# A graph layer's table build: four buffer places, x in seven groups, counts on two engines, stores on another queue

## The reference

```
f = layernorm(x) @ W_n                      # 6250 x 256, as 8 heads x 32
el, er = f . attn_l, f . attn_r             # per node 8 heads x 4 types
e  = leaky(((el[src] + er[dst] + edge16 . attn_m) . edge4) / 3)     # 200000 edges, sorted by dst
x  = x + segment_sum(f[src] * segment_softmax(e, dst), dst)
x  = x + mixture of 8 experts, best 2 of them, of layernorm(x)      # silu(h w1) * (h w3), w2
```

## Time and profile before

| what | us |
|---|---|
| median of 3 runs (4030.01 to 4046.42) | 4033.45 |
| the profiled execution, by its own time | 4042.06 |
| its span, first to last instruction | 4040.5 |
| VectorE, ACT, POOL, TensorE busy | 1992.2, 1598.6, 1860.2, 2976.2 |
| mean granted TensorE clock | 0.800 of full |

### The profile page before, as it was taken

One profiled execution on the slowest core, in us unless ns is written; L12 is line 12 of the kernel. 1 busy time (PEld: TensorE's weight loads), 2 busy tenths in 40 slices (PEclk: granted clock), 3 DMA queues, 4 the chain that ended last, 5 costly groups with the idle time before them and its releaser, 6 DMA issues. The chain is left out here.

```text
span 4040.5 us, 59260 instructions
## 1 busy us (share of the span) xinstructions
PE 2976.2 (74%) x12566; PEld 2283.4 (57%) x12567; DVE 1992.2 (49%) x5348; ACT 1598.6 (40%) x3631; POOL 1860.2 (46%) x1906
## 2 busy tenths in 40 slices
PE   2541677777777777767767777777665999999997
PEld 1221565555556666556555555656553677777775
DVE  5730566565655666556555565655782222222221
ACT  2310554544455455445445544544432222222221
POOL 0006466666666666666666666666163111111111
PEclk9765678787777777877778777767755999999998
DMA  7844444444445444444445444446555121121223
GB/s 219 269 140 115 116 135 134 131 136 135 132 135 145 133 133 134 135 132 135 134 134 143 135 135 132 134 134 123 120 188 176 31 31 31 31 31 31 31 31 83
DMA packets 309415, 481.35 MB, mean 119 GB/s; under 512 B 161911, under 2 KB 237507, under 8 KB 300366
## 3 DMA queue, kind: packets, MB, share of 16 engines
q0 software_dynamic: 100848, 285.40, 28.4%
q1 hardware_dynamic: 194910, 181.82, 14.9%
q10 hardware_dynamic: 13392, 11.23, 1.0%
HBM read 408.52 MB, written 76.12 MB: 120 GB/s over the span
## 5 line engine op out<-in xcount | busy, mean ns | idle before, releaser
L821 POOL DMA_INDIRECT rows<-table,idx x1664 | 1577.9, 948 | 981.3 <-issue 462.6
L864 PE MATMUL ps_acc<-rows,hot 128*128 128x264 f32 x3328 | 1217.8, 497 | 352.3 <-issue 158.2
L864 PEld LDWEIGHTS ps_acc<-rows,hot 128*128 128x128 f32 x3328 | 715.4, 238 | 456.3 <-issue 334.2
L849 PEld LDWEIGHTS ps_term<-er,hot_t 128*128 128x128 f32 x3328 | 607.2, 239 | 217.7 <-issue 155.1
L849 PE MATMUL ps_term<-er,hot_t 128*128 x3328 | 566.9, 300 | 91.3 <-issue 67.6
L1153 DVE TENSOR_TENSOR rows<-rows,ps_p 128x512 f32<-128x512 f32 x832 | 565.9, 680 | 6.0 <-ACT ps_p L973 0.5
L962 ACT ACTIVATE hot<-iota_row,neg_rel 128x128 f32<-128x128 f32 x1664 | 545.6, 388 | 5.5 <-PE ps_acc L864 5.5
L1736 PE MATMUL ps_h<-w,acc 128*128 x1680 | 528.5, 457 | 0.5 <-ACT acc L1655 0.5
L1648 POOL DMA_INDIRECT x_dram<-acc,to x105 | 161.8, 1541 | 761.9 <-ACT acc L1664 761.9
L1169 DVE TENSOR_TENSOR acc<-acc,ps_acc 128x264 f32 x832 | 354.9, 427 | 312.0 <-issue 171.4
L945 ACT ACTIVATE hot_t<-dst_row,neg_part 128x1024 f32<-128x1024 bf16 x208 | 235.6, 1133 | 520.4 <-remote 430.4
(11 more groups left out here) (263 smaller groups left out, 2827.1 us busy)
## 6 DMA issues: line engine op xcount, KB each, us to landing
dst_row<-rel_d SPq DMA_DIRECT2D x52, 1024.0 KB
rows<-table,idx POOLq DMA_INDIRECT x1664
rec<-rec_d SPq DMA_DIRECT2D x832, 24.0 KB
rec_d<-acc SPq DMA_DIRECT2D x16, 1050.0 KB
acc<-slots_x SPq DMA_DIRECT2D x105, 130.0 KB, 2.1
acc<-in_edge_attr_dram SPq DMA_DIRECT2D x16, 700.0 KB
wrow<-in_L_ffn_w_dram ACTq DMA_DIRECT2D x16, 640.0 KB
table<-fo SPq DMA_DIRECT2D x49, 148.0 KB
```

The lines of the kernel that those rows point to most:

```text
L821: pool.indirect_dma_start(rows[:, in_ring(k) + j, :], None, table, bass.IndirectOffsetOnAxis(ap=idx[w][:, t:t + 1], axis=0)).then_inc(gath ...
L849: last = pe.matmul(ps_term[s % 2][:, t * HT:(t + 1) * HT], hot_t[s % 2][:, t, :], flat(er[:, ds(b, 1), :]), start=False, stop=(t == QT - 1))
L864: last = pe.matmul(ps_acc[(k1 - 1) % SUM_BANKS][:, 0:PW], hot[m // QI % 2][:, m % QI * G + j, :], rows[:, in_ring(i * (2 * NI) + at) + j, ...
```

## The change

- `AHEAD` = 4 places for `xt`, `xn`, `fo` and `ps_f`, `TURNED` = 3 for `ps_t`, with waits that let each engine run as far ahead as there are places.
- x comes in seven groups of seven blocks (`load_x`), each with its own semaphore, statistics (`spread`), square root (`root`) and reciprocal (`roots`), the later ones inside the loop over blocks.
- The counts of odd blocks run on ACT: the sum over sign(thr - 0.5 - dst), which the next stage turns into a count by 0.5 s + 800. Those of even blocks stay on VectorE.
- Row stores and chunk stores are issued by POOL, on its own queue. SP's program holds loads alone; its order is x group 0, weights, router rows, dst, x group 1, src, chunks 0 and 1, x groups 2 to 6, chunks 2 to 15.
- One chunk for every three blocks (`chunk_after`).
- All loops are written out; before, they were loops of the engines' sequencers.

The diff, cut to its core:

```diff
-EARLY = 5
+AHEAD = 4
+TURNED = 3
+CHUNK_EVERY = 3
+ACT_COUNTS = range(1, BLOCKS, 2)
...
+            xt = sb(st, "xt", [P, AHEAD, KC, P])
+            xn = sb(st, "xn", [P, AHEAD, DIM])
+            fo = sb(st, "fo", [P, AHEAD, FD])
             ps_w = ps(st, "ps_w", [P, 512])
-            ps_t = [ps(st, f"ps_t{i}", [P, 512]) for i in range(2)]
-            ps_f = [ps(st, f"ps_f{i}", [P, 512]) for i in range(2)]
+            ps_t = [ps(st, f"ps_t{i}", [P, 512]) for i in range(TURNED)]
+            ps_f = [ps(st, f"ps_f{i}", [P, 512]) for i in range(AHEAD)]
...
+            def chunk_after(b):
+
+                c, left = divmod(b, CHUNK_EVERY)
+                return c if left == 0 and c < CHUNKS else None
...
+                    for b in range(BLOCKS):
+                        pool.wait_ge(f_sb, b + 1)
+                        pool.dma_start(table[b * P:(b + 1) * P, :], fo[:, b % AHEAD, :]).then_inc(f_out[b % AHEAD], 16)
+                        c = chunk_after(b)
+                        if c is not None:
+                            pool.wait_ge(rec_ok, c + 1)
+                            for part_of in SPREAD:
+                                pool.dma_start(rec_d[0:EDGES, :].rearrange("(p t) c -> p (t c)", p=EP)[part_of, c * CHUNK * RC:(c + 1) * CHUNK * RC],
+                                               rec_o[c % 2][part_of, :]).then_inc(rec_out[c % 2], 16)
+                    for u in range(AHEAD):
+                        pool.wait_ge(f_out[u], 16 * len(range(u, BLOCKS, AHEAD)))
+                    for u in range(2):
+                        pool.wait_ge(rec_out[u], 32 * (CHUNKS // 2))
...
+                    def load_x(g):
+
+                        lo, hi = g * BC, (g + 1) * BC
+                        if g == GROUPS - 1:
+                            hi -= 1
+                            sp.wait_ge(dve_step, 4)
+                            sp.dma_start(xall[0:LAST, hi, :], x[hi * P:NODES, :]).then_inc(x_in[g], 16)
+                        sp.dma_start(xall[:, lo:hi, :], x[lo * P:hi * P, :].rearrange("(b p) d -> p b d", p=P)).then_inc(x_in[g], 16)
+
+                    def load_chunk(c):
+                        u = c % 2
+                        if c >= 2:
+                            sp.wait_ge(rec_ok, c - 1)
+                        for tile, edge in ((e16_st[u], edge16), (e4_st[u], edge4)):
+                            f = edge.shape[1]
+                            for part_of in SPREAD:
+                                sp.dma_start(tile[part_of, :], edge.rearrange("(p t) f -> p (t f)", p=EP)[part_of, c * CHUNK * f:(c + 1) * CHUNK * f]).then_inc(chunk_in[u], 16)
+
+                    load_x(0)
+                    sp.dma_start(wall[:, :, 0:DIM], w_n.rearrange("(k p) d -> p k d", p=P)).then_inc(w_in, 16)
+                    sp.dma_start(rt_rows[:, :], router_w).then_inc(w_in, 16)
+                    sp.wait_ge(dst_none, 4)
                     sp.dma_start(dst_sb[0:1, 1:COLS + 1], dst[0:COLS].unsqueeze(0)).then_inc(dst_in, 16)
                     for lo, hi in ((1, 113), (113, EP)):
                         sp.dma_start(dst_sb[lo:hi, :], bass.AP(dst.tensor, lo * COLS - 1, [(COLS, hi - lo), (1, COLS + 1)])).then_inc(dst_in, 16)
-                    xv = x[0:(BLOCKS - 1) * P, :].rearrange("(b p) d -> p b d", p=P)
-                    sp.dma_start(xall[:, 0:BLOCKS - 1, :], xv).then_inc(x_in, 16)
-                    sp.dma_start(wall[:, :, 0:DIM], w_n.rearrange("(k p) d -> p k d", p=P)).then_inc(w_in, 16)
-                    sp.dma_start(rt_rows[:, :], router_w).then_inc(w_in, 16)
-                    sp.wait_ge(dve_step, 4)
-                    sp.dma_start(xall[0:LAST, BLOCKS - 1, :], x[(BLOCKS - 1) * P:NODES, :]).then_inc(x_in, 16)
+                    load_x(1)
...
+                    for c in range(2):
+                        load_chunk(c)
+                    for g in range(2, GROUPS):
+                        load_x(g)
+                    for c in range(2, CHUNKS):
+                        load_chunk(c)
...
+                    def root(g):
+
+                        act.wait_ge(var_ok, g + 1)
+                        act.activation(rstd[:, g * BC:(g + 1) * BC], mv[:, g * BC:(g + 1) * BC, 1], ACT.Sqrt, bias=eps[:, 0:1]).then_inc(std_ok, 1)
+
+                    root(0)
...
+                        if b >= AHEAD:
+                            act.wait_ge(f_ps, b - AHEAD + 1)
+                        act.copy(xt[:, b % AHEAD, :, :], ps_t[b % TURNED][:, 0:KC * P].rearrange("p (k n) -> p k n", k=KC)).then_inc(xt_sb, 1)
...
+                    def count(b):
+
+                        act.activation(junk_a, dst_sb[:, 1:COLS + 1], ACT.Sign, bias=thr_a[:, b:b + 1], scale=-1.0,
+                                       accum_out=cnt[:, b + 1:b + 2]).then_inc(signs_ok, 1)
+
+                    act.wait_ge(pad_ok, 2)
+                    act.dma_start(rec_d[EDGES:EDGES + PAD, :].rearrange("(a n) c -> a n c", a=64), pad_rec[:, :, :]).then_inc(pads, 16)
+                    copy_xt(0)
+                    copy_xt(1)
                     act.wait_ge(rec_zero, 2)
                     act.wait_ge(src_in, 32)
                     act.wait_ge(pen_ok, 1)
-                    copy_xt(0, 0)
-                    copy_xt(1, 1)
-                    for c in range(2):
-                        pack(0, c)
-                        for u in range(2):
-                            next_xt(2 * c + 2 + u, u)
-                    with act.Fori(1, CHUNKS // 2) as j:
-                        for c in range(2):
-                            pack(j, c)
-                            for u in range(2):
-                                next_xt(j * 4 + (2 * c + 2 + u), u)
-                    with act.Fori(2 * CHUNKS + 2, BLOCKS - 1, 2) as b:
-                        for u in range(2):
-                            next_xt(b + u, u)
-                    act.wait_ge(f_ps, BLOCKS - 2)
-                    copy_xt(BLOCKS - 1, 0)
+                    for b in range(BLOCKS):
+                        if b + 2 < BLOCKS:
+                            copy_xt(b + 2)
+                        if b % BC == 0 and b // BC + 1 < GROUPS:
+                            root(b // BC + 1)
+                        c = chunk_after(b)
+                        if c is not None:
+                            pack(c)
+                        if b in ACT_COUNTS:
+                            act.wait_ge(signs_ok, ACT_COUNTS.index(b))
+                            count(b)
...
+                    def spread(g):
+
+                        at = slice(g * BC, (g + 1) * BC)
+                        dve.wait_ge(x_in[g], 32 if g == GROUPS - 1 else 16)
+                        for b in range(g * BC, (g + 1) * BC):
+                            dve.bn_stats(stats[:, b, :], xall[:, b, :]).then_inc(stats_ok, 1)
+                        dve.wait_ge(stats_ok, BC * (g + 1))
+                        join_stats(dve, dve_steps, stats[:, at, :], mv[:, at, :], tmp[:, at, :], var_ok, g + 1)
+
+                    def roots(g):
+
+                        at = slice(g * BC, (g + 1) * BC)
+                        dve.wait_ge(std_ok, g + 1)
+                        dve_steps(dve.reciprocal(rstd[:, at], rstd[:, at]))
+
+                    def norm(b):
+                        if b >= AHEAD:
+                            dve.wait_ge(xt_ps, b - AHEAD + 1)
+                        dve.tensor_scalar(xn[:, b % AHEAD, :], xall[:, b, :], mv[:, b, 0:1],
+                                          rstd[:, b:b + 1], ALU.subtract, ALU.mult).then_inc(xn_ok, 1)
+
+                    def count(b):
+
+                        dve.tensor_scalar(junk[:, :], dst_sb[:, 1:COLS + 1], thr[:, b:b + 1], 0.0, ALU.is_lt, ALU.add,
+                                          accum_out=cnt[:, b + 1:b + 2]).then_inc(cnt_ok, 1)
+
+                    def rows_out(b):
+                        dve.wait_ge(f_ps, b + 1)
+                        if b >= AHEAD:
+                            dve.wait_ge(f_out[b % AHEAD], 16 * (b // AHEAD))
+                        to, got = fo[:, b % AHEAD, :], ps_f[b % AHEAD]
+                        dve.tensor_copy(to[:, 0:PW].rearrange("p (h d) -> p h d", h=HEADS)[:, :, 0:HDIM],
+                                        got[:, 0:DIM].rearrange("p (h d) -> p h d", h=HEADS))
+                        dve.tensor_copy(to[:, PW:FD], got[:, DIM:DIM + HT])
+                        dve.tensor_copy(er[:, b, :], got[:, DIM + HT:DIM + 2 * HT]).then_inc(f_sb, 1)
+
+                    spread(0)
+                    dve.wait_ge(dst_none, 4)
+                    dve_steps(dve.tensor_scalar(thr_a[:, :], thr_a[:, :], -0.5, None, ALU.add))
+                    roots(0)
+                    for b in range(AHEAD):
+                        norm(b)
...
+                    counted = 0
+                    for b in range(BLOCKS):
+                        if b + AHEAD < BLOCKS:
+                            norm(b + AHEAD)
+                        if b not in ACT_COUNTS:
+                            dve.wait_ge(cnt_ok, counted)
```

(62 more changed lines are left out.)

95 lines of the change are left out of this document (26 added, 69 removed).

## The result

The changed kernel takes 3987.99 us (median of 4 runs, 3982.85 to 3993.91) against 4033.94 for the kernel before in the same session: ratio 0.9877, interval 0.9858 to 0.9895, that is 46 us faster. 3976 was forecast, with 3952 to 4006 as range. The profiled execution took 3993.91 (span 3992.3) against 4042.06 (4040.5), 48.2 less.

What follows compares the result with a forecast made beforehand. DMA was taken to bound the table build where chunks are, start-up or VectorE elsewhere. 8 + 158.5 + 4.5 put its end at 171 instead of 230, 59 us less, giving 3976 us; range 3952 to 4006.

Steps and rivals of the forecast that it cites:

- Later stages unchanged: Behind the table build's barrier: later stages take as long as now, 2888 and 922 us, so its gain counts one to one.
- rival D: Edge stage: it gives the gain back through TensorE's clock, net 20 us or less, time 4015; chance 0.06.
- First block at 22.5: Table build's start: with x in groups and loads reordered, the first block starts at 22.5 us instead of 54.4.
- 32 us earlier: Table build's start: how much sooner the first block was to start, 22.5 instead of 54.4 us.
- 162 us of packets: Table build: DMA work of some 162 us within a stage of 230, the rest being holes.
- rival A: Table build's stores: POOL's queue stores slowly, at the gathers' 249 GB/s; stage 194 us, time 3997; chance 0.10.
- rival C: Chunk loop: packs wait for earlier chunk stores on POOL; loses from 13.2 us a chunk, time 4060 at 15; chance 0.04.
- Signs on ACT at 1.7 us, no swaps: Counts on ACT: 24 signs at 1.7 us each stay hidden, table swaps taken as 0 with 15 us kept for the range.
- so the 22.0 us go: Row stores: four outgoing buffers give a store three blocks' time, removing VectorE's 22.0 us wait for places.
- may stall it a microsecond each: Group statistics: VectorE's waits for ACT's roots, two blocks behind the join, may cost a microsecond each.
- rival B: ACT in order: packs or roots that wait hold xt copies; stage end 185, with swaps 200, time 3989 to 4004; chance 0.12.
- Nothing for POOL's queue but issue time: Stores on POOL: the move costs only 81 issues at 0.57 us, 46 us of an idle engine.

Runs made afterwards that it cites:

- e11: Changed kernel with all of x loaded and all statistics, roots and reciprocals taken before the first block; stage end 174.05 us, ratio 0.9871 to the kernel before.
- e2: Changed kernel with the eight attn_m loads on their own semaphore, so TensorE starts after 18 DMAs; stage end 181.79 us, ratio 0.9880 to the kernel before.
- e9: Changed kernel, stores on SP, attn_m semaphore apart, statistics ten blocks ahead, eight row places, x groups 3 to 6 between chunks; stage end 167.97 us, ratio 0.9862.
- e3: Changed kernel with row and chunk stores in SP's program again; stage end 175.42 us, ratio 0.9847 to the kernel before.
- e4: Changed kernel with 48 of 49 counts on VectorE, one on ACT; stage end 196.70 us, ratio 0.9906 to the kernel before.
- e6: Changed kernel with eight places for outgoing rows instead of four; stage end 176.97 us, ratio 0.9863 to the kernel before.
- e5: Changed kernel with each group's statistics ten blocks ahead of use instead of six; stage end 171.09 us, ratio 0.9831 to the kernel before.
- e7: Changed kernel with two places for xt, xn, fo, ps_t and ps_f; stage end 252.41 us, ratio 1.0079 to the kernel before.
- e1: Changed kernel with four extra POOL drains in its loop, at blocks 12, 24, 36 and 44; stage end 184.40 us, ratio 0.9873 to the kernel before.
- e8: Changed kernel with a chunk every second block instead of every third; stage end 192.39 us, ratio 0.9933 to the kernel before.
- a0: Changed kernel itself, unedited, run again on a faster chip; stage end 182.28 us, ratio 0.9868 to the kernel before.

## Why the prediction was right or wrong

The forecast of 3976 was 12 us too low, and its reason, a stage that DMA bounds and whose holes close, held: of the 68 us that the stage was longer than its packets' time (230 - 162) 26 are left (182 - 156). By its own steps:

- **Later stages unchanged: right.** 3810.3 us from tri to the end in both. The clock of the edge stage is 0.75 instead of 0.74, and nothing was given back (rival D).
- **First block at 22.5: wrong, it was 34.17.** The small loads were put at 3 to 6 us behind their issue, by the pad store's 6.3. They were issued by 13.86 and landed at 29.88, 16 us later. Full DMA engines alone don't explain it: they were as full in the kernel before (1.04 from 8 to 22), where behind dst only x and the weights stood beside them, and the pad store behind them landed in 6.3; and as full in e11 (1.04), where x groups stand beside them again and they land 5 us behind their last issue. In the changed kernel and in e2 and e9 (15 us) src and the two first chunks are issued beside them, from 8.7 to 14.5. That these hold them up is the likely cause; no run moves them alone. The failed step carried nothing: e2 takes it away and the stage end stays. "32 us earlier" was never a term of the time, since the sum goes by DMA; what the earlier start fed was the emptiness of 35 to 55 us, and for this the loads need only be issued, not the first block turned. e11 shows it from the other side.
- **162 us of packets: 6 too many.** They took 156.5. The stores, put at 84 us (317 GB/s), took 73 (365 GB/s), near the 383 of the forecast's lower bound, and rival A fell; its 249 GB/s was q0's whole traffic, not only the gathers'. The loads took 83 where rival C has 77. The Trainium skill (DMA: Bandwidth & Descriptors, Rules for kernel authors) says that spreading over queues gives no bandwidth. The runs don't contradict it: with the stores on SP (e3) the share is 0.93 instead of 0.85 from 100 to 150, packets take 162 us, and the stage is shorter by the drain. With two queues the same bytes took 153 to 162, so those 6 us can't be put down to the number of queues.
- **Signs on ACT at 1.7 us, no swaps: right.** The sign took 1.635 us and 0.197 for reading its sum, 1.83 together. One table load stands in the stage and no swap, so root and sign share a table here. The 15 us kept for swaps weren't needed. e4 prices the move at 14 us.
- **"so the 22.0 us go": wrong, 21.1 stayed.** A row takes 8.0 us to land on a full DMA, three blocks' time, so four places are just too few; with eight the wait is gone (e6).
- **The root, which "may stall it a microsecond each": wrong, and of the steps that count this is the one that failed.** The stall was sought on VectorE, and stood on ACT: 31.1 us in six, up to 7.4. The root of the next group is in ACT's program at a block's start, VectorE joins the statistics for it behind row copies that wait for stores, and all xt copies and packs stand behind the root. That is one half of rival B, whose stage end of 185 is nearer to 182 than the forecast's 171; its other half, packs that wait for chunks, which its price was worked out from, fell to 7.6 us. e5 takes the roots' waits away: 11.2 us.
- **Nothing for POOL's queue but issue time: wrong by a term that was missing.** The DRAIN at the barrier, 6.68 us behind 81 DMAs, stands on the path that sets the stage end.
- **Rival C: no.** Three blocks with their chunk took (171.9 - 34.2) x 3/49 = 8.4 us, as forecast, and far under the 13.2 from which C decides. e7 loses to the kernel before, but by too few places.

The books: forecast 171; drain +6.7; packets -6; the rest, about +10, is what is left over for the holes of ACT's roots and row places. That makes 182. The missing drain and the 6 us too many of packets cancel, and that is luck: e5, without the roots' holes but with the drain, gives 171.09, the forecast's own number, by these two errors. How the ten split between roots and places stays open, as e5 and e6 act on the same chain.

## What to carry to other kernels

Find the floor of the stage first (packets' time), and then price every wait by what it empties: the 12 us later start cost nothing, statistics that came too late for a root on an in-order engine 11. Statistics that another engine finishes for you belong a whole group ahead, not two blocks. Stores that move to POOL's queue also bring POOL's drain at the next barrier, which SP's queue did not have.

## What the runs showed of the hardware

- POOL's DRAIN at the barrier, which in this stage begins when all stores have landed, takes 0.62 us with 7 since the last drain, 0.71 with 8, 6.68 with 81 (the same in all ten profiles with the 81 stores on POOL and no drain between) and 8.06 with 98: some 0.08 us for each from 7 on. Where it issued none it took 0.82, early in the stage. Behind the 1664 gathers of the edge stage the rule doesn't hold: 14.8 us in the kernel before, 24.2 in the changed one. Among stores in flight it takes 7.3 to 8.8 behind 14 to 20 (e1). SP's takes 7 ns behind the same 81 stores (e3).
- The stage's 51 MB took 162 to 165 us of packets' time with everything on SP's queue (the kernel before, e3, e9), and 153 (e8, e11) to 162 us (e7) with the stores on POOL's. The number of queues alone doesn't set it.
- ACT's 24 small loads (0.5 to 2 KB each, 2000 packets with the pad store) landed 15 to 16 us behind their issue with src and chunk loads beside them (the changed kernel, e2, e9), and 5 us behind their last issue with x groups instead (e11), the DMA engines being full in both.
- An ACT operation with a running sum costs a further 197 ns for its reading; the copy of the same size took 1524.
- The kernel before took 4034 and 4037 us in two sessions and 3573 to 3574 on two other chips, and the changed kernel's table build took the same on both chips that it ran on. The groups of the gathers, of the changed kernel on the chip of the result and then on a0's, show where it went:

```profile
L834 POOL DMA_INDIRECT rows<-table,idx x1664 | 1578.3, 948 | 981.0 <-issue 457.0 <-remote 250.8 <-PE ps_acc L877 220.6
```

```profile
L834 POOL DMA_INDIRECT rows<-table,idx x1664 | 1574.0, 946 | 532.8 <-issue 475.4 <-PE ps_acc L877 31.4 <-DVE idx L1082 26.1
```

The gathers are issued equally fast, but POOL idles 448 us more ahead of them on the former, 220.6 of it (31.4 on the other) for TensorE's products (496 ns each there, 478 on the other) and 250.8 for something that the profile only calls remote. Its cause wasn't looked for. It is no part of this change, as it lies behind the barrier in both kernels.
